# The half-row products of the down projection grouped over two pairs of tiles

## The reference

```
x = x + attention(layernorm(x))
x = x + ffn(layernorm(x))
ffn(x) = sum over the 4 chosen of 16 experts of  w_e * (silu(x Wg_e) * (x Wu_e)) Wd_e     (inner width 192)
         + the same with one shared expert for every token, without a weight
```

## Time and profile before

| What | Value |
|---|---|
| median of three runs | 1948.24 us (1952.13, 1948.24, 1946.98) |
| span of the profiled execution | 1946.1 us |
| PE busy | 1871.1 us, 96% |
| DVE, ACT, POOL busy | 53%, 50%, 47% |
| mean clock of PE | 0.987 of full |

### The profile page before, as it was taken

The page is one execution under the profiler, slowest core; times in us unless marked ns, Lnnn a source line. Parts: engine busy times, 40 slices in busy tenths (PEclk is TensorE's granted clock), DMA queues, the critical chain, the costliest instruction groups (busy, mean ns, idle before and its releaser), DMA issues.

```text
span 1946.1 us, 34880 instructions
## 1 busy us (share of the span) xinstructions
PE 1871.1 (96%) x9240; PEld 963.5 (50%) x9241; DVE 1030.1 (53%) x1995; ACT 980.6 (50%) x1917; POOL 921.2 (47%) x1127
## 2 busy tenths in 40 slices
PE   6799999999999999999999999999999999999996
PEld 5444445444544454445333455555555555555553
DVE  5667777878788878877887152222211222222213
ACT  3366776777677766776776532222332233322330
POOL 3532566666666766674643550333333333333342
PEclk9899999999999999999999999999999999999998
DMA  6423233534353335333542797877777777777779
GB/s 193 117 62 85 70 94 125 155 99 107 125 156 99 105 127 155 98 95 117 145 153 86 256 342 232 183 141 141 142 142 143 142 141 141 143 144 141 142 165 260
DMA packets 159128, 277.71 MB, mean 143 GB/s; under 512 B 28704, under 2 KB 64800, under 8 KB 156256
## 3 DMA queue, kind: packets, MB, share of 16 engines
q1 hardware_dynamic: 108688, 147.61, 27.2%
q0 software_dynamic: 40880, 106.96, 26.8%
q10 hardware_dynamic: 9440, 21.68, 3.2%
HBM read 145.65 MB, written 135.74 MB: 145 GB/s over the span
## 4 chain that ended last, share of the span: by engine, by line
PE 83%; ACT 5%; DMA 4%; DVE 3%; issue 2%; POOL 1%; SPq 1%; DVEq 0%; POOLq 0%
PE ps_gu L1911 22%; PE ps_pv L1210 12%; PE ps_exp L1197 10%; PE ps_max L1183 9%; PE ps_y L1930 7%; PE ps_misc L1103 5%; PE ps_y L1934 4%; PE ps_x L1890 4%; ACT prob L723 3%; DVE mx L973 2%; PE ps_misc L1128 2%; PE ps_misc L1152 2%; DMA wts_sb<-second_sum_rows 1%; PE ps_misc L1223 1%; PE ps_misc L1074 1%
## 5 line engine op out<-in xcount | busy, mean ns | idle before, releaser
L973 DVE TENSOR_REDUCE mx<-ps_max 128x2 f32<-128x1024 f32 x512 | 617.6, 1219 | 169.5 <-PE ps_max L1183 155.4
L723 ACT ACTIVATE prob<-ps_exp 128x512 f32<-128x512 f32 x1024 | 584.0, 597 | 152.9 <-PE ps_exp L1197 135.2
L1197 PE MATMUL ps_exp<-qs,ks 98*128 98x512 bf16 x1024 | 391.3, 383 | 23.0 <-ACT prob L723 19.8
L1911 PE MATMUL ps_gu<-wts_sb,xT 128*128 x1152 | 402.7, 493 | 1.5 <-issue 1.5
L1610 POOL DMA_INDIRECT out<-yt,idx x72 | 111.7, 1551 | 468.4 <-ACT yt L1679 453.9
L1183 PE MATMUL ps_max<-ks,qs 96*128 96x512 bf16 x1024 | 308.0, 382 | 8.0 <-DVE mx L973 4.4
L1791 DVE COPY hT<-ps_h 128x384 f32<-128x384 f32 x88 | 49.0, 557 | 464.0 <-PE ps_h L1920 464.0
L1911 PEld LDWEIGHTS ps_gu<-wts_sb,xT 128*128 128x128 f32 x1152 | 207.3, 190 | 171.1 <-issue 56.7
L1210 PE MATMUL ps_pv<-prob,vs 128*32 128x512 f32 x2048 | 253.3, 608 | 0.0
L1669 ACT ACTIVATE gs<-ps_gu 128x192 f32<-128x192 f32 x176 | 58.2, 330 | 376.7 <-PE ps_gu L1911 376.7
L1197 PEld LDWEIGHTS ps_exp<-qs,ks 98*128 98x128 bf16 x1024 | 99.5, 97 | 209.2 <-ACT prob L723 99.7
(11 more groups left out here) (191 smaller groups left out, 2146.8 us busy)
## 6 DMA issues: line engine op xcount, KB each, us to landing
xt<-rows_by_expert SPq DMA_DIRECT2D x144, 264.5 KB, 2.7
dnr_sb<-in_dnr SPq DMA_DIRECT2D x144, 128.0 KB, 2.6
qk_parts<-parts POOLq DMA_DIRECT2D x112, 120.0 KB, 3.6
qs<-qk_parts SPq DMA_DIRECT2D x64, 192.0 KB, 3.1
wts_sb<-in_wts ACTq DMA_DIRECT2D x12, 1024.0 KB, 7.6
x_sb<-in_x SPq DMA_DIRECT2D x16, 512.0 KB, 4.6
qs<-qk_parts SPq DMA_DIRECT2D x64, 128.0 KB, 3.1
x_plus_memory<-am SPq DMA_DIRECT2D x16, 512.0 KB, 5.3
```

Of the source, the lines that this page charges most:

```text
L723: act.activation(prob[:, s, q], ps_exp[:, q % 2], ACT.Exp, scale=SCALE).then_inc(s_exp, 1)
L973: dve.tensor_reduce(mx[:, k % 2, 4 * s + 2 * p:4 * s + 2 * p + 2], ps_max[:, p], AX_X, ALU.max).then_inc(s_maxd, 1)
L1197: pe.matmul(ps_exp[:, q % 2], ks[0:ROWS + MROWS, kk, s * P:(s + 1) * P], qs[0:ROWS + MROWS, kk, q], start=True, stop=True).then_inc(s_sc, 1)
L1911: mm = pe.matmul(ps_gu[:, i, 0:2 * I], xT[:, i, d], w, start=(d == 0), stop=(d == DC - 1))
```

## The change

In the change, pairs from B0 = H0 - 2 = 8 up to H1 - 1 = 81 are `together`: the down projection of an even pair does only its two 128-row products (into banks 0 and 1 of y), and that of the odd pair after it does its own two (banks 2 and 3) and then all four half-row products, the even pair's first (`down_rest`). Bank 3 of y is the attention's `ps_misc`. The other pairs keep the order of before. So y of both pairs is complete at the same time: ACT's `y_out` copies four tiles in a row in the even body after, and POOL adds them from there. `hT` gets two buffers.

The banks come from `ps_x`, which keeps one. So the transposes of x are split: tile 0 of pair h + 1 goes right behind the transposes of the hidden, before the second gate_up, and tile 1 behind the second gate_up as before; ACT copies each in turn. SP loads the rest of the down weights of two pairs (four DMAs) in the even body.

```
--- before.py
+++ after.py
@@ -1302,12 +1302,12 @@
     done = {"xn2_stored": [(s_xn2st[r], 16 * (NU // 2)) for r in range(2)], "x2_stored": [(s_x2st, 16 * NU)],
             "x_added": [(s_xa, NU)], "xm_stored": [(s_xmst, 16 * NU)], "logits": [(s_lg, NU)], "cleared": [(s_clear, 16 * 3)],
             "scattered": [(s_sct[r], 2 * K * 16 * (NU // 2)) for r in range(2)], "parts": [(s_parts, 2 * NU)],
-            "relu": [(s_rl, 2 * NU)], "qk_stored": [(s_qk[n], QK_DMAS[n] * (NU - 2)) for n in range(3)],
+            "relu": [(s_rl, 2 * NU)], "misc_free": [(s_misc, NU + 1)], "qk_stored": [(s_qk[n], QK_DMAS[n] * (NU - 2)) for n in range(3)],
             "projected": [(s_proj, 4 * NU)], "scores": [(s_sc, 16 * NG)], "pv": [(s_pv, 4 * NG)], "o_transposed": [(s_otp, NG)],
             "maxima": [(s_maxd, 8 * NG)], "exp": [(s_exp, 16 * NG)], "oT": [(s_oT, NG)], "elu": [(s_sig, 2 * NU)],
             "memory_read": [(s_amp, MEM * NU)], "shared_weights": [(s_ws, 48)], "o_added": [(s_x2, 2 * NU)],
             "xn2_early": [(s_xn2st[r], 16 * ((NU - 1 - r) // 2)) for r in range(2)]}
-    return {"sync": sync, "gpsimd": gpsimd, "scalar": scalar, "vector": vector, "tensor": tensor, "done": done}
+    return {"sync": sync, "gpsimd": gpsimd, "scalar": scalar, "vector": vector, "tensor": tensor, "done": done, "misc": ps_misc}
@@ -1325,6 +1325,7 @@
     H1 = H0 + NR // 2
     H2 = H1 + LATE // 2
     W = DC * 2 * I + D
+    B0 = H0 - 2
     POOL_PADS = 4
     PIECES = [[(0, slice(0, I))], [(2 * P, slice(0, P)), (I, slice(P, I))]]
     ZERO_ROW = sizes(T)[1]
@@ -1354,8 +1355,7 @@
     yt = lent("yt", [P, 4, D])
     gs = lent("gs", [P, 2, I])
     hid = lent("hid", [P, 2 * I])
-    hT = lent("hT", [P, 3, P])
-    lent("room_in_qf", [P, P])
+    lent("room_in_qf", [P, 4 * P])
     onehot = lent("onehot", [P, NR, E])
     lent("room_in_parts", [P, 3200 - NR * E])
     dnr_sb = lent("dnr_sb", [P, 2, D])
@@ -1369,8 +1369,10 @@
     jrow = room[:, NR * E:NR * (E + 3)].rearrange("p (k j) -> p k j", k=3)
     jt = room[:, NR * (E + 3):NR * (E + 9)].rearrange("p (k j) -> p k j", k=6)
-    ps_x = own.enter_context(nc.psum_tensor("ps_x", [P, 2, DC, P], F32))
-    ps_y = own.enter_context(nc.psum_tensor("ps_y", [P, 2, D], F32))
+    ps_x = own.enter_context(nc.psum_tensor("ps_x", [P, DC, P], F32))
+    ps_y = own.enter_context(nc.psum_tensor("ps_y", [P, 3, D], F32))
+    ps_misc = heads["misc"]
+    hT = keep["hT"]
     ps_gu = own.enter_context(nc.psum_tensor("ps_gu", [P, 2, D], F32))
     ps_h = own.enter_context(nc.psum_tensor("ps_h", [P, DC, P], F32))
@@ -1424,8 +1426,15 @@
             self.t = None if self.kind == ROUTED else [(h if h < H0 else h - (H1 - H0)) * 2 + i for i in range(2)]
             self.routed = h - H0
+            self.together = not known or B0 <= h < H1
+
         def slot(self, i):
             return 2 * self.par + i
+
+    def y_of(pair, i):
+
+        bank = 2 * pair.par + i if pair.together else i
+        return ps_misc[:, :] if bank == 3 else ps_y[:, bank]
     L0, L1 = H0 + 6, H1 - 2
@@ -1442,6 +1451,12 @@
                 body(*around(r * 2 + (L0 + i), r + L0 // 2, i))
         for h in range(L1, H2):
             body(*around(h, h // 2, h % 2))
+
+    def whole(pair):
+
+        if not pair.exists or pair.together and pair.par == 0:
+            return []
+        return [Pair(pair.h - 1, pair.q, 0), pair] if pair.together else [pair]
     def rows_of(dram, t):
         return dram[bass.ds(t * P, P)]
@@ -1532,12 +1547,13 @@
                 if is_at(pair, 5 + n):
                     for e in range(POOL_PADS + 6 * n, POOL_PADS + 6 * n + 6):
                         pad(e)
-            if is_at(following, H0):
+            if is_at(pair, H0):
                 all_of("xm_stored")
-            if following.exists and following.kind == ROUTED:
-
-                after(wait, s_yp, following.h - 1)
+            if pair.par == 0 and pair.kind == ROUTED:
+
+                wait(s_yp, pair.h)
+                load_rest(pair)
                 load_rest(following)
         first = [Pair(h, 0, h) for h in range(2)]
@@ -1655,12 +1671,11 @@
             join(t, s_join[1])
     def scalar(act):
-        def x_out(pair):
-            for i in range(2):
-                act.wait_ge(s_xp, 2 * pair.h + i + 1)
-
-                after(act.wait_ge, s_gu, 2 * pair.h + i - 1)
-                act.activation(xT[:, i], ps_x[:, i], ACT.Copy).then_inc(s_xT, 1)
+        def x_out(pair, i):
+            act.wait_ge(s_xp, 2 * pair.h + i + 1)
+
+            after(act.wait_ge, s_gu, 2 * pair.h + i - 1)
+            act.activation(xT[:, i], ps_x[:], ACT.Copy).then_inc(s_xT, 1)
         def silu(pair, i):
             act.wait_ge(s_gu, 2 * pair.h + i + 1)
@@ -1676,7 +1691,7 @@
                     after(act.wait_ge, s_yst[pair.slot(i)], 16 * pair.q)
                 else:
                     act.wait_ge(s_add[i], 16 * (pair.routed - 1))
-                act.activation(yt[:, pair.slot(i)], ps_y[:, i], ACT.Copy).then_inc(s_y, 1)
+                act.activation(yt[:, pair.slot(i)], y_of(pair, i), ACT.Copy).then_inc(s_y, 1)
         def store(pair):
             for i in range(2):
@@ -1705,15 +1720,19 @@
         def body(before, pair, following, later):
             silu(pair, 0)
+            if following.exists:
+                x_out(following, 0)
             last_units(chain, pair, "a")
             silu(pair, 1)
             if following.exists:
-                x_out(following)
+                x_out(following, 1)
             last_units(chain, pair, "b")
-            if before.exists and not before.both:
-                y_out(before)
-            if before.exists and before.kind == SHARED and not before.late:
-                store(before)
+            for ready in whole(before):
+                if not ready.both:
+                    y_out(ready)
+            for ready in whole(before):
+                if ready.kind == SHARED and not ready.late:
+                    store(ready)
             if before.both:
                 store_late(before)
             last_units(chain, pair, "c")
@@ -1725,7 +1744,8 @@
             for s, n in done[name]:
                 act.wait_ge(s, n)
                 act.sem_inc(s_acg, 1)
-        x_out(Pair(0, 0, 0))
+        for i in range(2):
+            x_out(Pair(0, 0, 0), i)
         pairs(act, body)
         end = Pair(H2 - 1, (H2 - 1) // 2, (H2 - 1) % 2)
         act.wait_ge(s_y, 2 * end.h + 2)
@@ -1787,8 +1807,8 @@
         def hT_out(pair):
             dve.wait_ge(s_hp, pair.h + 1)
-            after(dve.wait_ge, s_yp, pair.h)
-            dve.tensor_copy(hT[:], ps_h[:, 0:3]).then_inc(s_hT, 1)
+            after(dve.wait_ge, s_yp, pair.h - 1)
+            dve.tensor_copy(hT[:, pair.par], ps_h[:, 0:3]).then_inc(s_hT, 1)
         def weights(pair):
@@ -1838,7 +1858,7 @@
             dve.wait_ge(s_yp, pair.h + 1)
             dve.wait_ge(s_both, n)
             for i in range(2):
-                dve.tensor_tensor(late_y(pair, i), ps_y[:, i], sums[:, n, i], ALU.add).then_inc(s_y, 1)
+                dve.tensor_tensor(late_y(pair, i), y_of(pair, i), sums[:, n, i], ALU.add).then_inc(s_y, 1)
         def body(before, pair, following, later):
             if before.exists:
@@ -1880,15 +1900,14 @@
         y_sum(end)
     def tensor(pe):
-        def transpose_x(pair):
-            for i in range(2):
-                slot = pair.slot(i)
-                pe.wait_ge(s_x[slot], 16 * pair.q + 16)
-
-                after(pe.wait_ge, s_xT, 2 * pair.h + i - 1)
-                for d in range(DC):
-                    mm = pe.transpose(ps_x[:, i, d], xt[:, slot, d * P:(d + 1) * P], identf[:])
-                mm.then_inc(s_xp, 1)
+        def transpose_x(pair, i):
+            slot = pair.slot(i)
+            pe.wait_ge(s_x[slot], 16 * pair.q + 16)
+
+            after(pe.wait_ge, s_xT, 2 * pair.h + i)
+            for d in range(DC):
+                mm = pe.transpose(ps_x[:, d], xt[:, slot, d * P:(d + 1) * P], identf[:])
+            mm.then_inc(s_xp, 1)
         def experts(pair):
@@ -1922,16 +1941,27 @@
         def down(pair, es):
             pe.wait_ge(s_hT, pair.h + 1)
-            after(pe.wait_ge, s_y, 2 * pair.h)
+            if pair.together and not is_at(pair, B0):
+                pe.wait_ge(s_y, 2 * (pair.h - 1))
+            else:
+                after(pe.wait_ge, s_y, 2 * pair.h)
+            if is_at(pair, B0 + 1):
+
+                for s, n in done["misc_free"]:
+                    pe.wait_ge(s, n)
+            for i in range(2):
+                w = sdn_sb[:] if pair.kind == SHARED else of_expert(es[i], slice(W - D, W))
+                pe.matmul(y_of(pair, i), hT[:, pair.par, i], w, start=True, stop=False)
+            for ready in whole(pair):
+                down_rest(ready)
+
+        def down_rest(pair):
             if pair.kind == ROUTED:
                 pe.wait_ge(s_dn[pair.par], 32 * (pair.q - H0 // 2) + 32)
             for i in range(2):
```

(14 more changed lines are left out.)

## The result

| | before | after |
|---|---|---|
| median of five runs | 1950.12 us (1946.98 to 1952.13) | 1992.07 us (1987.93 to 1996.15) |
| profiled execution, span | 1946.1 us | 1994.3 us |
| PE busy, 1300 to 1850 us | 549.82 | 524.22 |

The ratio of the times is 1.0226 [1.0212, 1.0239]: 42 us slower, where 7.3 were forecast and the range ended at 1968. The profiled execution after is the slowest of its five, 4.1 us over their median.

The account below looks back on a forecast made before the run. PE was taken to bound the middle and the last indirect add the end; -14.8 + 0.4 + 15.8 + 5.9 = +7.3 us on the 1946.1 span gave 1953.4, plus 2.1 for the runs' median 1955.5 us, range 1941 to 1968.

Parts of the forecast that it names:

- The saving: Half-row products in the routed pairs: one switch in and out saved per group, 37 x 0.40 us, -14.8 us.
- What costs nothing on PE: ACT's copies, hidden buffers, single x bank, SP's rest loads: free on PE except +0.4 us at the very start.
- How long that landing takes: Odd pairs' loads of x take 3.2 us (2.7 to 3.5), so PE waits 0.44 in 36 groups: +15.8 us.
- the third add: Extra indirect add per group, issued at +7.3 to +7.9 us after the halves, its packets starting while x moves.
- a sign of being wrong: The third add meeting the start of the load of x, making it longer than 3.5 us.
- The room of 2.76 us: From an odd body, PE waits once a group for what the landing of x takes above 2.76 us.
- The end: Last indirect add lands 14.3 us after the last halves instead of 8.4, delaying the final sums: +5.9 us.
- The sum in the loop: Loop share of the saving and the wait for x; whole-kernel sum was -14.8 + 0.4 + 15.8 + 5.9 = +7.3 us.
- Signs named ahead: Half-product records 1.9 us, x waits 0.2 to 0.7, two loading times, PE 97 to 98% busy, last add 14 us.
- the rivals: Load little disturbed, 1948.3 (chance 0.27); switch pays, 1939.7 (0.20); change doesn't do what it says, 1963 (0.07).

Follow-up runs that it names:

- e8_third_add_later: Third and fourth add of a group held until the next body's first transposes of x are done, against the changed kernel with early table loads: 1955.81 us, a single run.

## Why the prediction was wrong

- **The saving** (-14.8): right to the rounding, 0.40 us a group, 32 x 0.40 in the loop. The four steps of the halves take 1.92 us, which is 4 x 0.43 and one switch in of 0.20.
- **"What costs nothing on PE"**: this is the step that failed first. It priced the single bank at nothing because 2.58 us of gate_up lie between tile 1's transposes and ACT's copy of tile 0. That holds for the engine and not for its sequencer, which stops at the wait and can't prepare what comes behind it: branch, four table loads, gate_up. It was priced at 0 and costs 1.08 us at each of the loop's 31 jumps back, 34 us in all. The text had looked at PE's work alone; "issue" in front of the weight loads in the earlier trace rows was read as the price of switching between half and whole rows only.
- **"How long that landing takes"**: the mechanism was right (the third add), and the size was wrong: 3.2 us forecast, 3.5 the upper bound, 3.9 to 4.0 measured. The bound was the longest load that the trace of before held, and no load there had the add in that place. The place was wrong too: the first add was taken to be issued 1.77 us behind the halves, as before, and is issued 0.90 behind them, so that the third comes at +6.6 and not at +7.3 to +7.9, and its packets meet the start of the load. The prediction had named that as a sign of being wrong, and it came. The true wait would be 1.22 a group, not 0.44; in the kernel after only 0.22 of it shows, since the gap before the even body's first gate_up gives the load another 1.08 us. Without the gap that term alone, 32 x 1.22 = 39 us for 14, would have put the kernel beyond the range: 1991.08 with the table loads moved.
- **The room of 2.76 us**: right to a tenth, by the sum above. The load is issued 2.1 us behind the gate_up, as taken, and from the landing to the first transpose it is 0.13 us (taken at 0.2).
- **The end** (+5.9): +6.6 from the halves to the last landing, right in kind and a little small. The stretch grew by 6.8.
- **Not priced at all**: one load of 9.13 us while the experts' weights still come in, 6 us of PE, and 2 us more of waiting for x in body 7.
- **The sum in the loop**: forecast -12.8 + 14.1 = +1.3, measured +26.7. By the parts it is 32 x (-0.40 + 0.22) for the saving and the load, 31 x 1.08 for the gap and 0.21 at the exit, +27.9, less the 1.2 that before's loop had over 64 x 9.34: +26.7.
- **Signs named ahead**: the half-product records (1.9), the last add (15.1 for 14) and two values of the loading time came; PE's busy share in the middle was to be 97 to 98% and is 95.3%, and the idle time for x of 0.2 to 0.7 was right in place, with more idle time elsewhere. Of the rivals none had the sequencer in it.

The hold at the copy is shown by the event 0.06 us behind it in every turn, by its following the copy when that moves, and by the gap's going when the table loads do. The grouping with two banks for x was not tried: y of two pairs takes four banks, and in this kernel none is free. Open is why the first table load after the jump back takes 0.3 to 0.4 us in some kernels and 0.7 to 0.8 in others. It goes with the hardware queue's packets: in the five kernels where that queue is nearly idle in the 0.6 us around the start of this load (under 0.15 of the DMA engines' time) it is short, in the nine where it takes 0.34 to 0.42 it is long. That is a coincidence in time, and no run tests it.

## What to carry to other kernels

A wait that is hidden from an engine may not be hidden from its sequencer: count what lies behind it until the next instruction that the engine needs (branches, address loads, register work), and set against it the work still queued at that point; regrouping work into every second body takes that cover from the other one. Where a transfer moves towards others, the spread seen so far bounds nothing, and two limits that are nearly equally late must be lifted together before either shows its worth. Here that made 1.0226 into 0.9962.

## What the runs showed of the hardware

- The first table load of PE's sequencer after the loop's back edge takes 0.37 us in the median before, 0.70 after, 0.30 in the two kernels with SP's order of before and ungrouped halves, 0.32 with the adds held (`e8_third_add_later`), and 0.7 to 0.8 in the others that are grouped or load the rest four at a time; the branch takes 0.22 when taken and 0.08 at the loop's exit.
- From the loop's branch to the first step of the next gate_up PE's sequencer takes 4.1 to 4.3 us with four table loads in between and 2.3 to 2.8 with two (medians of the kernels here); where PE waits for it, the gate_up starts 4.3 to 4.4 us behind the branch. A body has to leave that much in products at the branch.
- PE's sequencer does nothing behind transposes that wait until they are released: its next step comes 0.06 us after ACT's copy and 0.04 us after DVE's.
- With one more indirect add of 128 rows, issued 1.5 us ahead of it, a load of x of 264.5 KB a tile takes 4.0 us; with that add and the next held back it takes 2.7 (a single run), and with two loads of 128 KB moved away from it instead 3.9 (a single run).
